# Four fused transformer parts: the barriers between the parts replaced by one fixed, interleaved order of steps

## What is computed

```
x = x + _L0_xattn_ref(_layernorm(x), ctx_2048, ctx_2048)                  # part a
x = x + _L0_ffn_ref(_layernorm(x), L0_ffn_w1, L0_ffn_w2)                  # part b
x = x + _L1_xattn_ref(_layernorm(x), ctx_2048, Wq, Wk, Wv, Wo, ...)       # part c
x = x + _L1_ffn_ref(_layernorm(x), L1_ffn_w1, L1_ffn_w2, L1_ffn_w3)       # part d

# part b: rows and weights are quantised, 256 -> 1024 -> 256
h = gelu(gelu(bitlinear158(x, w1)));  return bitlinear158(h, w2)
# part c: 16 query heads, 4 key heads of 128; keys are 128 of ctx and the 128 rows themselves
q = rope(rms_norm(x @ Wq.T));  k = rope(rms_norm(kv_in @ Wk.T));  v = kv_in @ Wv.T
x_out = (softmax(q @ k.T * SCALE) @ v) @ Wo.T
# part d: quantised as in b, 256 -> 704 -> 256, gated
return bitlinear(silu(bitlinear(x, w1)) * bitlinear(x, w2), w3)
```

## Time and profile before

| quantity | value |
|---|---|
| median of 3 timed runs | 791.6 us (790.96 to 792.22) |
| the profiled execution | 793.7 us |
| its span from first to last instruction | 791.7 us |
| PE, DVE, ACT, POOL busy | 661.8, 668.3, 625.3, 521.1 us |
| granted PE clock, mean | 0.942 |
| barriers in the span | 168.9, 242.5 and 711.4 us |

### The profile page before, as it was taken

The page is one execution under the profiler, slowest core; times in us unless marked ns, Lnnn a source line. Parts: engine busy times, 40 slices in busy tenths (PEclk is TensorE's granted clock), DMA queues, the critical chain, the costliest instruction groups (busy, mean ns, idle before and its releaser), DMA issues. The chain is left out here.

```text
span 791.7 us, 16306 instructions
## 1 busy us (share of the span) xinstructions
PE 661.8 (84%) x4660; PEld 387.7 (49%) x4660; DVE 668.3 (84%) x1668; ACT 625.3 (79%) x2103; POOL 521.1 (66%) x705
## 2 busy tenths in 40 slices
PE   2688788846755689999999999999999999875776
PEld 0233333312333356666666666666666666542443
DVE  4889758568972799999999999999999999858995
ACT  2578878739972799999999999999999999835551
POOL 4666665335753887787887788778878887503553
PEclk9989989669995999999999999999999999998996
DMA  7556766402451469878878886797788879730445
GB/s 287 147 156 166 207 166 200 126 7 56 92 101 20 94 121 163 138 134 141 145 138 129 151 147 135 127 155 139 133 147 140 138 129 162 139 59 17 81 95 129
DMA packets 308521, 102.05 MB, mean 129 GB/s; under 512 B 285392, under 2 KB 303952, under 8 KB 308176
## 3 DMA queue, kind: packets, MB, share of 16 engines
q1 hardware_dynamic: 308432, 101.02, 63.4%
HBM read 22.33 MB, written 8.39 MB: 39 GB/s over the span
## 5 line engine op out<-in xcount | busy, mean ns | idle before, releaser
L1232 ACT ACTIVATE psum<-psum,arena 128x256 f32<-128x256 f32 x256 | 136.0, 531 | 19.7 <-DVE arena L1348 19.7
L1304 DVE SCALAR_TENSOR_TENSOR arena<-psum,arena 128x256 f16<-128x256 f32 x256 | 111.0, 475 | 0.5 <-ACT arena L1249 0.5
L1249 ACT ACTIVATE arena<-psum,arena 128x256 f16<-128x256 f32 x256 | 100.6, 476 | 4.1 <-DVE arena L1317 1.2
L1394 PE MATMUL psum<-wq_t,arena 128*128 128x512 f16 x384 | 94.6, 383 | 10.2 <-DMA arena<-arena 6.7
L1186 POOL TENSOR_TENSOR arena<-arena 128x512 f32<-128x512 f32 x64 | 81.4, 1271 | 31.2 <-DVE arena L1323 31.1
L1426 PE MATMUL psum<-arena 128*128 128x512 f16 x384 | 93.6, 379 | 5.4 <-DVE arena L1331 5.4
L1438 PE MATMUL psum<-wo_t,arena 128*128 128x256 f16 x768 | 95.5, 275 | 0.1
L1416 PE MATMUL psum<-arena 128*128 128x256 f16 x768 | 94.3, 273 | 1.2 <-DMA arena<-arena 1.0
L825 ACT ACTIVATE arena<-psum 128x1024 f32<-128x1024 f32 x64 | 65.7, 1029 | 27.6 <-PE psum L981 27.5
L1438 PEld LDWEIGHTS psum<-wo_t,arena 128*128 128x128 f16 x768 | 75.4, 98 | 23.2 <-DVE arena L1331 0.4
L1323 DVE TENSOR_TENSOR arena<-psum,arena 128x1024 f32<-128x1024 f32 x64 | 78.4, 1225 | 6.6 <-PE psum L1394 6.6
(11 more groups left out here) (169 smaller groups left out, 1597.9 us busy)
## 6 DMA issues: line engine op xcount, KB each, us to landing
split_scratch<-arena SPq DMA_DIRECT2D x48, 128.0 KB, 2.0
arena<-split_scratch SPq DMA_DIRECT2D x32, 192.0 KB, 4.0
arena<-arena SPq DMA_TRANSPOSE x272, 3.3
arena<-in_ctx SPq DMA_DIRECT2D x16, 256.0 KB, 3.6
x_rows<-in_x SPq DMA_DIRECT2D x4, 512.0 KB, 9.3
arena<-in_b_w SPq DMA_DIRECT2D x2, 1024.0 KB, 8.6
arena<-in_wq SPq DMA_DIRECT2D x4, 512.0 KB, 5.7
arena<-in_wo SPq DMA_DIRECT2D x4, 512.0 KB, 5.5
```

Of the source, the lines that this page charges most:

```text
L1232: last = eng.activation(s_banks(u)[:, h, :], s_banks(u)[:, h, :], ACT.Exp, bias=bias[:, u % 2, h:h + 1], scale=r_q(u)[:, h:h + 1], accum_o ...
L1249: hi = eng.activation(p_hl[:, u % 2, 0, h, :], s_banks(u)[:, h, :], ACT.Copy, scale=share[:, u % 2, h:h + 1])
L1304: last = eng.scalar_tensor_tensor(p_hl[:, u % 2, 1, h, :], s_banks(u)[:, h, :], share[:, u % 2, h:h + 1], p_hl[:, u % 2, 0, h, :], ALU.mul ...
L1394: mm = eng.matmul(Q_BANK, y_t[:, b % 2, x, k, :], c.wq_t[:, w, k, SHARE * P * g:SHARE * P * g + SHARE * P], start=(n == 0), stop=(n == 5))
```

## The change

The barriers between the parts are gone; one is left at the end. Each engine's function of a part is now a generator that stops (`yield`) at the head of every step, and a new function, `steps`, runs the generators of the four parts in the fixed order of the table ORDER, the same on all five engines. An entry such as ("b", 2) lets part b run on to its next two stops. So the last eleven steps of a alternate with b0 to b3, the steps b12 to b25 alternate with c0 to c9, and the last seven steps of c alternate with d0 to d3; everything else stands as it stood.

What makes this possible: buffers are put into regions of the arena (which grows from 20 to 23 Ki words) so that parts that overlap don't overlap in memory; c's query and key banks in PSUM move from 0 and 1 to 6 and 7, its attention and output banks from 6 and 7 to 0 and 1. New waits stand where a part first uses what its neighbour made or leaves: b's statistics of batch t wait for a's two adds of that batch (`given`), c's statistics for b's sum of that batch, d's for c's; the first wide and the first narrow product (`first_wide`, `first_down`), c's first scores, first attention, first probabilities and their transposes wait until the part before has finished with the place.

Two things change in the work itself. c's first two batches and units get their inverse roots from POOL's power instead of ACT's logarithm and exponential, and ACT's table for these is loaded in c6. And each batch of c has one more DVE operation, variance plus epsilon (`var`), which was an addend of ACT's logarithm before.

```
-    def new_part(self):
-        self.used = 0
+    def region(self, first, last):
+        self.used, self.limit = 256 * first, 256 * last
...
-def part_ffn(core, name, up, gate, down, x_dram):
+def part_ffn(core, name, up, gate, down, x_dram, early, late, given, each, first_wide, first_down):
...
     def vector(eng):                       # part_ffn
         for s in range(STEPS + 1):
+            yield
...
             t = tile(s, 0)
             if t is not None:
+                eng.wait_ge(given, each * (t + 1))
                 eng.bn_stats(stats[:, t % 2, :], c.x_rows[:, t, :]).then_inc(S["stats"], 1)
...
     def tensor(eng):                       # part_ffn
             t = tile(s, INNER)
             if t is not None:
+                if t == 0:
+                    eng.wait_ge(*first_wide)
...
     def pool(eng):                         # part_c
+            b = batch(s, ROWS)
+            if b is not None and b < 2:
+                eng.wait_ge(S["stats"], 3 * (b + 1))
+                wait(eng, S["y"], b)
+                eng.tensor_tensor(rstd[:, :], var[:, :], c.minus_half[:, 0:1], ALU.pow).then_inc(S["rstd"], 2)
...
+                if u < EARLY:
+                    eng.wait_ge(S["r"], 2 * u + 1)
+                    eng.tensor_tensor(r[:, u % 8, :], log_ms[:, :], c.minus_half[:, 0:6], ALU.pow).then_inc(S["r"], 1)
...
     def scalar(eng):                       # part_c
-        eng.preload_act_table_set("natural_log_exp_and_others")
...
+            if s == PROJ + EARLY:
+                eng.preload_act_table_set("natural_log_exp_and_others")
...
-                eng.activation(log_var[:, :], mv[:, 1:2], ACT.Ln, bias=eps[:, 0:1]).then_inc(S["rstd"], 1)
+                eng.activation(var[:, :], var[:, :], ACT.Ln).then_inc(S["rstd"], 1)
...
     def vector(eng):                       # part_c
             b = batch(s, 0)
+                eng.wait_ge(ffn["out"], b + 1)
                 eng.bn_stats(stats[:, :], c.x_rows[:, b, :]).then_inc(S["stats"], 1)
...
                 eng.bn_aggr(mv[:, :], stats[:, :]).then_inc(S["stats"], 1)
+                eng.wait_ge(S["stats"], 3 * b + 2)
+                eng.tensor_scalar(var[:, :], mv[:, 1:2], LN_EPS, None, ALU.add).then_inc(S["stats"], 1)
...
+ORDER = (("a", 76), ("b", 2), ("a", 3), ("b", 1), ("a", 3), ("b", 1), ("a", 3), ("b", 1), ("a", 2), ("b", 8),
+         ("c", 1), ("b", 1), ("c", 1), ("b", 1), ("c", 1), ("b", 1), ("c", 1), ("b", 1), ("c", 1), ("b", 1),
+         ("c", 1), ("b", 2), ("c", 1), ("b", 2), ("c", 1), ("b", 1), ("c", 1), ("b", 1), ("c", 1), ("b", 3),
+         ("c", 59), ("d", 2), ("c", 2), ("d", 1), ("c", 2), ("d", 1), ("c", 2), ("d", 1), ("c", 1), ("d", 24))
...
+        def steps(eng, n):
+            engines = {name: part[n](eng) for name, part in parts.items()}
+            for name, count in ORDER:
+                for _ in range(count):
+                    next(engines[name], None)
...
+            barrier(eng)
```

More of the change, by code:

```diff
@@ L152, in part_ffn @@
     SLOTS = 6
-    yc = c.local("yc_" + name, [P, 2, D])
+    c.region(*late)
     act1 = c.local("act1_" + name, [P, 2, WIDE])
@@ L157, in part_ffn @@
     junk = c.local("junk_" + name, [P, WIDE])
+    q2_t = c.local("q2t_" + name, [P, 3, CHUNKS2, P], F16)
+    c.region(*early)
+    yc = c.local("yc_" + name, [P, 2, D])
     q1 = c.local("q1_" + name, [P, 2, D], F16)
@@ L436, in tensor @@
             if t is not None:
+                if t == 0:
+                    eng.wait_ge(*first_down)
                 if t >= 2:
@@ L1057, in tensor_weights @@
         return step
+    c.opened = S["added"]
     return sync, pool, scalar, vector, tensor
@@ L1270, in scalar @@
                 eng.activation(v[:, u % 8, 0, :, :], kv_view[:, :, 1, :], ACT.Copy).then_inc(S["v_hi"], 1)
+            if u is not None and u >= EARLY:
                 eng.wait_ge(S["ss_q"], u + 1)
@@ L1289, in scalar @@
             u = unit(s, PROJ)
-            if u is not None:
+            if u is not None and u >= EARLY:
                 eng.wait_ge(S["r"], 2 * u + 1)
@@ L1354, in vector @@
                 u, b = proj, proj // GROUPS
+                if u < EARLY:
+                    eng.wait_ge(S["ss_q"], u + 1)
+                    eng.wait_ge(S["ss_k"], u + 1)
+                    wait(eng, S["r"], 2 * u)
+                    eng.tensor_scalar(log_ms[:, :], sums[:, u % 2, :], 1.0 / HEAD_DIM, 1e-6 * W_SCALE * W_SCALE,
+                                      ALU.mult, ALU.add).then_inc(S["r"], 1)
                 eng.wait_ge(S["r"], 2 * (u + 1))
@@ L1411, in tensor @@
             if u is not None:
+                if u == 0:
+                    eng.wait_ge(ffn["gelu"], BATCHES)
                 eng.wait_ge(qk_turned[u % 2], 16 * (u // 2 + 1))
@@ L1419, in tensor @@
             if u is not None:
+                if u == 0:
+                    eng.wait_ge(ffn["out"], BATCHES)
                 eng.wait_ge(p_turned[u % 2], 32 * (u // 2 + 1))
@@ L1472, in _ @@
             constants_pool(eng)
-            for (_, pool, _, _, _), barrier in parts:
-                pool(eng)
-                barrier(eng)
+            steps(eng, 1)
         @block.scalar
         def _(eng):
-            for (_, _, scalar, _, _), barrier in parts:
-                scalar(eng)
-                barrier(eng)
+            steps(eng, 2)
         @block.vector
@@ L1485, in _ @@
             eng.wait_ge(core.consts_ready, 6)
-            for (_, _, _, vector, _), barrier in parts:
-                vector(eng)
-                barrier(eng)
+            steps(eng, 3)
         @block.tensor
         def _(eng):
-            for (_, _, _, _, tensor), barrier in parts:
-                tensor(eng)
-                barrier(eng)
+            steps(eng, 4)
 def laid_out(inputs):
```

95 lines of the change are left out of this document (59 added, 36 removed).

## The result

The changed kernel takes 780.27 us (median of 4 runs, 779.7 to 781.79) where the kernel before takes 791.91 beside it: a ratio of 0.9853, 95% interval 0.9825 to 0.9881. That is 11.6 us less. The forecast was 22.3 less, and the time lies 1.3 us above the upper end of the range. The direction was right and the size was half.

What follows compares the result with a forecast made beforehand. No engine is full overall; steady c is full, so only emptying and filling at three seams can win. 4.6 + 15.1 + 5.0 - 2.4 = 22.3 off 791.6 gives 769.3 us, range 765 to 774 (chance 0.52).

Steps and rivals of the forecast that it cites:

- Seam a to b: Where b starts behind a: ACT's first gelu comes earlier, a gain of 4.6 us, bounds 3 and 6.
- Seam b to c: Where c starts beside b's tail: c's rows from c10 on come 15.1 us earlier, bounds 11 and 18.5.
- The lengths of c's steps: Seam b to c: c4 5.85, c5 5.4, c6 5.2 us on DVE, their waits on ACT filled by b's steps.
- 0.5 is put on c4 for POOL's power: Seam b to c: computing c's early powers on POOL lengthens step c4 by 0.5 us.
- PE has idle time there: Seam b to c, before c4's product: PE has idle time and early transposes, so DVE was let be last.
- Steady c: Dense part of c: one extra DVE operation per batch, 14 by 0.17, loses 2.4 us, bounds 0 and 3.4.
- The fourth rival: Steady c: softmax bias collides with POOL, 0.54 by 56 units, 30 us lost, 799 us; chance 0.05.
- the 0.1 at which the prediction had called itself wrong: Steady c: the prediction is wrong if c's period changes by over 0.1 us a unit.
- Seam c to d: Where d's first steps move into c's tail: a gain of 5.0 us after 3.4 lost, bounds 2.5 and 7.5.
- The ports: Interleaved stretches: DVE operations slower beside POOL could cost up to 4.5 us; nothing taken off; as rival 774, chance 0.09.
- Of the rivals the first: Seam b to c: in-order queues eat 6.7 of the 15 us as c and b steps keep waits, 776; chance 0.18.
- The prediction's own mark of failure: Seam b to c: wrong if DVE's waits on ACT or PE from 216 to 270 sum to over 5 us.

Runs made afterwards that it cites:

- seq: The changed kernel with its parts run one behind the other, nothing interleaved, still without barriers: 799.62 us, 1.0112 of the kernel before.
- bc: The changed kernel with only the seam b to c interleaved, the rest one part after the other: 786.36 us, 0.9942 of the kernel before.
- cd: The changed kernel with only the seam c to d interleaved, the rest one part after the other: 793.61 us, 1.0019 of the kernel before.
- novar: The changed kernel without the extra DVE operation of c after the second batch; ACT's logarithm adds epsilon again: 775.06 us, 0.9776 of the kernel before.
- order4: The changed kernel with c4 and c5 cut in two, the early powers' scale on POOL and b's last steps placed later: 774.4 us, 0.98 of before.
- again: The changed kernel unchanged, run a second time as a reference: 780.12 us, 0.985 of the kernel before.
- guard: The changed kernel with DVE's wait for POOL's constants moved from the part's first step to the step using them: 777.9 us, 0.9834 of before.

## Why the prediction was too good

**Seam a to b (4.6): right.** Last mixing to first gelu fell by 5.61, less the 1.45 that the last mixing pays: 4.2 net. `seq`, `bc` and `cd`, which have no barrier but the old order, stand at 11.30 for this distance, so 1.6 of it are the barrier and the table load and 4.0 the order.

**Seam b to c (15.1): wrong, and the reason for the miss.** It brought 3.67, 11.4 less than forecast. The terms of the forecast (from its own starts) and what they measured:

| stretch | forecast | after | `bc` | `novar` | `order4` |
|---|---|---|---|---|---|
| first gelu to c's first product on DVE | 41.8 | 43.20 | 42.99 | 42.95 | 42.95 |
| from there to unit 0 | 28.8 | 34.28 | 32.42 | 32.35 | 31.63 |
| unit 0 to unit 3 | 23.7 | 28.27 | 25.32 | 25.06 | 21.36 |

Three of its steps failed. The first is "The lengths of c's steps are taken from the earlier trace rows ... with waits on ACT in them that the b steps now fill". No step of b filled them: in c4 and c5 DVE waits 3.25 and 3.30, where it waited 2.46 and 2.76, and c4, c5 and c6 took 6.6, 6.5 and 7.0 (5.9 in `bc`) instead of 5.85, 5.4 and 5.2. A step of b fills a wait inside a step of c only if it stands there in DVE's queue; it stood behind the whole step. The order of the rows after c6, shown ahead of the prediction, already said it: a whole step of c between two of b. At b's end, unit 0 to unit 2 was put at 15.6 and took 19.0 (17.4 in `bc`): there b's last narrow products wait on PE for DVE (3.67 at 264.88) with c's query product behind them.

The second is "0.5 is put on c4 for POOL's power". `seq`, which interleaves nothing, needs 4.2 more than before up to unit 0 and 4.6 up to unit 4. The term had POOL's operation in it, but not that DVE itself must wait for ACT's squares to scale them and then once more for POOL, nor that PE runs at the lower clock level behind the longer waits.

The third was put at nothing: PE's clock, in a stretch of which the forecast said that "PE has idle time there". With the same order of steps b to c took 112.47, 112.39 and 112.18 in the changed kernel, `again` and `guard`, but 107.47 and 107.06 in `bc` and `novar`. The windows of 62 us from 40 us behind the first gelu on (columns as in the earlier trace rows: stretch, length, busy time of PE, PEld, DVE, ACT, POOL with counts, granted clock of PE, DMA share, GB/s), of the changed kernel and of `novar` (`bc` has 0.92 too):

```profile
210.93:272.93 62.00, 44.69 (x256) 28.18 (x255) 45.09 (x113) 37.25 (x138) 45.05 (x58) 0.81 0.50 89
```

```profile
213.37:275.37 62.00, 43.42 (x283) 28.63 (x281) 48.85 (x122) 41.78 (x154) 48.13 (x62) 0.92 0.56 98
```

In the changed kernel PE is busy longer with fewer products, so more of the stretch lies at the lower level of 1.2 GHz. `guard` and `novar` show where they part. For 65 us from the first gelu on, the rows of DVE, ACT and POOL agree to 0.03 us. PE of `guard`, then of `novar` (first gelu at 174.23 and 173.37):

```profile
236.84 0.39 PE L452 MATMUL psum<-cs_b,minus_off 128*128 128x256 f16 x1 [4.51 <-DVE x_rows L361]
...
238.73 2.76 PE L1448 MATMUL psum<-wq_t,arena 128*128 128x512 f16 x6
...
243.30 1.47 PE L1472 MATMUL psum<-arena 128*128 128x256 f16 x12
...
255.10 1.51 PE L1448 MATMUL psum<-wq_t,arena 128*128 128x512 f16 x6 [2.64 <-ACT arena L1302]
...
260.41 2.77 PE L1472 MATMUL psum<-arena 128*128 128x256 f16 x12
```

```profile
235.96 0.39 PE L452 MATMUL psum<-cs_b,minus_off 128*128 128x256 f16 x1 [4.50 <-DVE x_rows L361]
...
237.85 1.91 PE L1451 MATMUL psum<-wq_t,arena 128*128 128x512 f16 x6
...
240.91 1.47 PE L1475 MATMUL psum<-arena 128*128 128x256 f16 x12
...
251.89 1.46 PE L1451 MATMUL psum<-wq_t,arena 128*128 128x512 f16 x6 [1.73 <-ACT arena L1303]
...
255.98 1.47 PE L1475 MATMUL psum<-arena 128*128 128x256 f16 x12
```

In both, PE stands still for 4.5 us until DVE's sum releases b's narrow product, and its next products run at the lower level. In `novar` the upper level is back after some 2.7 us, within the six query products (1.91); in `guard` after some 5.7, so these take 2.76 and the scores begin 1.5 us later behind the first gelu (69.07 against 67.54). DVE waits for the scores, ACT for DVE, and then PE for ACT: 2.64 in `guard`, 1.73 in `novar`. Behind that longer wait and one more for DVE, PE falls to the lower level a second time, and the twelve scores take 2.77; in `novar` they take 1.47. The changed kernel does as `guard` (266.77 above is a third such place, 2.77 for six query products that take 1.46 at 273.77), `bc` as `novar`. So a slower PE lengthens the waits, and the longer wait was followed by a second fall of the clock. Why the clock came back 3 us later in the one than in the other was not found: from 10 us behind the first gelu to that point no row of PE differs by more than 0.4 us between the two.

By the runs, then, the 11.4 are: 4.1 that the start of c costs without any interleaving above the 0.5 (`seq`), 5.0 that the changed kernel lacks against `bc` in the same order of steps, and 2.3 by which the interleaving itself (13.3 in `bc` against `seq`) stays under the 15.6 that the forecast had for it, waits unfilled and b's end together. `order4`, which cuts c4 and c5, gives POOL the scale and places b's end anew, wins 9.8 back; how much of that each of the three and the clock brought is open.

**Steady c (2.4): the mechanism right, the size off.** The forecast's term was 14 batches by 0.17; it measured 0.33 each and 4.66 in all (4.3 to 4.9 in the profiles that keep the operation), outside its bounds of 0 to 3.4. The 0.17 was the extra operation alone. The other half is the softmax start that it pushes into POOL's cast. The fourth rival had this phase between POOL and DVE in mind, for another operation and every unit; it came in one unit of four, at 0.18. In the mean that is 0.08 a unit, just under the 0.1 at which the prediction had called itself wrong.

**Seam c to d (5.0): right.** 3.06 lost and 8.61 won, 5.5 net (in `again` 7.0 won, 4.0 net). Of the 3.06, `guard` removed 1.9 with the wait for POOL's constants.

**The ports** were taken at nothing, with 4.5 as their price if not. Small DVE operations in the interleaved stretch did get longer beside POOL: L338 took 0.78 at 223.29, where its line of before took 0.17 at 225.66. How much of the 11 us these are is not separated. The Trainium skill, page "SBUF — State Buffer", section "Who interferes with whom", says that VectorE and GpSimd share a pair of ports under an exclusive lock. The rows agree in kind, in the seam (0.78 beside a POOL operation of 1.12 at 222.94) and in the steady part (0.32 beside the cast).

**The sum.** By the profiles the four terms are 4.2 + 3.7 - 4.7 + 5.5 = 8.7 (4.6 + 15.1 - 2.4 + 5.0 forecast). The medians differ by 11.6; of the rest, 1.6 can be part a, which in the profile of before stands 1.6 behind the mean of the other kernels, and 1.3 is in no seam. Of the rivals the first, that the in-order queues eat the gain (776), was nearest, and it put the time 4.3 too low. Half of its condition is what the rows show: the steps of c keep their waits. The other half is not: from b17 to b21 DVE waits for nothing in b's steps. The prediction's own mark of failure, over 5 us of waits on ACT or PE from 216 to 270 on DVE, is what the rows show: 11.8.

## What to carry to other kernels

Where two pipelines are interleaved in one fixed order, a wait is filled only by work that stands between the producer's release and the waiting instruction in that engine's own queue; so cost a merged step as its own length with all its waits, engine by engine, and count on the neighbour only where its work stands inside the wait. Where the first pipeline ends, look at what stands behind its last products in PE's queue. Price a new wait on PE's side too: a wait that leaves PE idle can bring its next products to the lower clock level, and that was the largest single piece here (5.0 of 11.4). An operation added to the dense part is paid in each period, and was paid twice over here, because it moved its neighbour beside an operation of POOL; look there first when the steady part got longer. Put a wait at the first instruction that needs it, not at the head of the part.

## What the runs showed of the chip that was not expected

The same order of steps had two lengths, 112 us (three profiles) and 107 us (two) from b's first gelu to c's unit 4, with PE's granted clock at 0.81 and 0.92. Two of these kernels ran alike for 65 us and had PE idle for the same 4.5 us; then its clock came back to the upper level after 2.7 us of products in the one and after 5.7 in the other, and 5 us hung on that.

A DVE operation of 128x4 took 0.14 when it began just before POOL's cast of 0.40 and 0.31 or 0.32 when it began 0.1 behind it, in 13 of 13 places each; in the latter it ends with the cast (463.96 and 463.94).

ACT's table load cost its 1.28 us only where nothing covered it: at 165.58 it ended 4 us ahead of the first gelu.
